# The last block of a feed-forward kernel: pieces of tiles, where small sums run, and who adds the residual

## The chip, the cores and the metric

The kernel runs on the 8 cores of one Trainium2 chip, each with its own half of one batch element; the cores don't exchange data. The metric is the device time of the slowest core in microseconds (us). A core has five engines with a queue of instructions each, worked off in order: TensorE (PE in the profile, PEld its weight loads), VectorE (DVE), ScalarE (ACT), GpSimd (POOL) and SyncE (SP). Sixteen DMA engines move data between HBM and SBUF; transfers are issued from the queues of SP, GpSimd or ScalarE. Matmuls write into PSUM, which has 8 banks of 128 x 512 float32. An instruction waits on semaphores that other engines count up.

## The reference, cut to what matters

```
x   = x + LN(attention(LN(x)))          # called x1 below
x   = x + LN(ffn(LN(x)))
ffn(x) = (silu(x gate_w' * gate_s) * (x up_w' * up_s)) down_w' * down_s
LN(x)  = (x - mean) / sqrt(var + 1e-5)
```

Rows have 2048 columns and the inner width is 5632. Each core holds 1024 rows. The change is in the last line alone: the product with down_w, the scale down_s, the layer norm of each row and the addition of x1.

## The kernel before, in words

The 1024 rows of a core are 8 tiles (`tt` 0 to 7) of 128 rows. After attention, x1 of each tile is written to the output tensor `y` in HBM (`x1`, L505, `spill`), and its layer norm is kept in SBUF. The feed-forward part then goes over 44 slices of 128 of the inner width (`gi`), in ten blocks: nine of 4 slices and a last one of 8 (`BLKS`). For a slice the gate and up products are made (L799), joined and gated into `hdn`. Then `down` multiplies `hdn` with the slices of down_w for each tile (`down_mm`, L830, the matmul at L837) into four banks of PSUM, and VectorE adds these 2048 columns to the float32 accumulator `acc` in SBUF (`acc_add`, L852).

In the last block (from L935) the down products of all 8 tiles follow one another: 8 slices x 4 banks = 32 matmuls a tile, bank after bank (`by_bank`), tiles 0, 2, 4, 6 into banks 0 to 3, the others into banks 4 to 7. Behind each tile come:

- `acc_add`: VectorE adds PSUM to `acc`;
- `scaled` (L970): VectorE multiplies by down_s (`dsB`) and sums the row (`accum_out`), one instruction with two SBUF operands and a short read of the accumulator;
- `squares` (L978): ScalarE squares the row and sums it; the written squares go to `junk`, so that one waits for the other;
- `means` (L986): VectorE makes minus the mean and minus the squared mean, 128 x 1 each; `variance` (L996): VectorE adds the mean square;
- `rstd` (L1002): ScalarE takes logarithm and exponential of the variance; `bias` (L1009): VectorE makes the bias, which holds the constant `cN` of the first layer norm;
- `normed` (L1015): ScalarE normalises the tile in place, 2048 wide;
- `add_up` (L1022): GpSimd issues an accumulating DMA that adds the tile to x1 in `y`.

The order on each queue is the order in which the program calls these helpers. For a tile `tt` below 6 (loop at L1050) `variance` and `rstd` of tile `tt - 1` stand ahead of `scaled(tt)`, and `bias`, `normed` and `add_up` of `tt - 1` behind `means(tt)`.

Tiles 6 and 7 are treated apart (from L1068). `part(tt, k)` adds, scales and squares one quarter, 512 columns, as soon as its bank is done. The four partial sums are added by `joined` and `joined_sq` (`reduce_sum` on VectorE). x1 of these two tiles has been read back from `y` into `x1r` (two DMAs on SP's queue, L962, when the last gate product is done); VectorE adds it and SP writes the sum (`store`, L1029). Tile 6 goes in two halves, tile 7 in four quarters. On VectorE's queue, the first half of tile 6's `store` stands ahead of `joined(7)`, and the second ahead of `bias(7)`. The last instruction of the program waits for all writes.

## Time and profile before

| | |
|---|---|
| median of 3 runs | 1055.78 us (1053.21 to 1227.72) |
| profiled execution | 1055.02 us, span of its slowest core (core 7) 1053.5 us |
| spans of the 8 cores | 1049.5 to 1053.5 us |
| busy: PE, DVE, ACT, POOL | 96%, 56%, 27%, 5% of the span |
| chain that ended last | PE 81%, DMA 5%, DVE 5%, ACT 5%, issue 3% |

The span goes from the first to the last instruction or transfer of a core; the 1.5 us that the execution is longer lie around it. Busy shares are means over stages with different limits. The chain of waits is followed back from what ended last, at each step to what released it. A wait is put down to the engine whose signal came last. In the timeline each row has start, duration, engine, line, operation, and, in brackets, how long the engine stood idle before it and for whom. ACT's and DVE's short READ_ACCUMULATOR instructions belong to the sums ahead of them.

### The profile page before, as it was taken

What the parts mean: (1) busy time and instruction counts of PE and PEld (TensorE: products, weight loads), DVE (VectorE), ACT (ScalarE), POOL (GpSimd) and SP (SyncE); (2) the same over time, 40 slices, a digit from 0 to 9 for tenths busy, and PEclk for the clock granted to TensorE, in tenths of its full rate; (3) what the DMA queues carried; (4) which work ended last, traced back from release to release, by engine and by line L of the source; (5) the groups of instructions that cost most, each with busy time, mean ns of one, the idle gap of its engine ahead of it and who ended that gap; (6) DMA issues with size and microseconds to landing.
All of it is one profiled execution on the core that took longest, in us unless ns stands there. A gap on an engine that the chain in (4) does not pass through costs nothing.

```text
span 1053.5 us, 12922 instructions; the slowest of 8 cores (1049.5 to 1053.5 us)
## 1 busy us (share of the span) xinstructions
PE 1006.6 (96%) x4868; PEld 461.8 (44%) x4868; DVE 591.6 (56%) x814; ACT 289.5 (27%) x427; POOL 52.1 (5%) x98
## 2 busy tenths in 40 slices
PE   2899999999999999999999999999999999999993
PEld 0345554444444444444444444444444444444441
DVE  3656667445646555654655555654555555555577
ACT  3555666622112012111112112111112121112266
...
GB/s 210 144 1 110 113 138 50 149 162 81 46 69 79 116 52 87 114 41 104 97 40 123 77 40 147 54 40 159 41 53 147 40 73 128 49 71 162 119 120 200
DMA packets 18636, 101.35 MB, mean 96 GB/s; under 512 B 2192, under 2 KB 2320, under 8 KB 9744
## 3 DMA queue, kind: packets, MB, share of 16 engines
...
q8 instruction: 40, 0.66, 0.3%
...
## 4 chain that ended last, share of the span: by engine, by line
PE 81%; DMA 5%; DVE 5%; ACT 5%; issue 3%; POOL 0%; DVEq 0%; ACTq 0%; SPq 0%; POOLq 0%
PE ps L799 45%; PE ps L837 28%; PE ps L443 4%; DMA dwb<-dw 3%; PE ps L412 2%; DMA wr<-gu 1%; DVE xr L508 1%; ACT lc L545 1%; DMA xr<-xtop 1%; ACT lc L468 1%; ACT pc L334 1%; PE ps L732 1%; ACT bop L340 1%; DVE acc L826 0%; DVE att L426 0%
## 5 line engine op out<-in xcount | busy, mean ns | idle before, releaser
L799 PE MATMUL ps<-bop,wr 128*128 128x512 bf16 x2352 | 520.0, 379 | 1.7 <-DMA wr<-gu 1.7
L799 PEld LDWEIGHTS ps<-bop,wr 128*128 128x128 bf16 x2352 | 229.9, 98 | 279.3 <-issue 2.5
L837 PE MATMUL ps<-dwb,hdn 128*128 128x512 bf16 x1344 | 307.2, 379 | 1.0 <-DMA dwb<-dw 0.9
L852 DVE TENSOR_TENSOR acc<-acc,ps 128x2048 f32<-128x2048 f32 x70 | 160.2, 2288 | 213.2 <-PE ps L837 213.2
L837 PEld LDWEIGHTS ps<-dwb,hdn 128*128 128x128 bf16 x1344 | 131.3, 98 | 160.5 <-issue 2.9
L772 ACT COPY tmp<-ps 128x512 f32<-128x512 f32 x126 | 73.3, 582 | 347.7 <-PE ps L799 347.7
L780 DVE TENSOR_TENSOR tmp<-tmp,ps 128x512 f32<-128x512 f32 x126 | 86.5, 686 | 92.1 <-ACT tmp L772 46.0
L759 DVE TENSOR_TENSOR wr<-wr 128x1024 bf16<-128x1024 bf16 x168 | 114.2, 686 | 8.2 <-DMA wr<-gu 3.7
L443 PE MATMUL ps<-att,xT 128*128 128x512 bf16 x512 | 117.4, 379 | 0.5 <-DVE xT L341 0.5
L710 ACT ACTIVATE sg<-tmp,cpks 128x512 bf16<-128x512 f32 x63 | 45.5, 722 | 239.7 <-DVE tmp L780 239.7
L443 PEld LDWEIGHTS ps<-att,xT 128*128 128x128 bf16 x512 | 49.5, 98 | 58.2 <-issue 1.0
L86 POOL DMA_DIRECT2D wr<-gu x44 | 23.5, 534 | 888.9 <-PE ps L799 625.6
L721 DVE SCALAR_TENSOR_TENSOR hdn<-tmp,cpks,sg 128x512 bf16<-128x512 f32 x63 | 47.3, 751 | 6.6
L412 PE MATMUL ps<-V,Xn 128*128 128x512 bf16 x128 | 36.2, 395 | 4.5 <-DVE att L426 1.9
L850 DVE COPY acc<-ps 128x2048 f32<-128x2048 f32 x8 | 18.3, 2292 | 25.4 <-PE ps L837 25.4
L721 DVE SCALAR_TENSOR_TENSOR hdn<-ps,cpks,sg 128x512 bf16<-128x512 f32 x25 | 18.6, 749 | 23.4 <-PE ps L799 11.1
L426 DVE TENSOR_SCALAR att<-ps 128x1024 bf16<-128x1024 f32 x16 | 19.6, 1225 | 19.8 <-PE ps L412 19.8
L710 ACT ACTIVATE sg<-ps,cpks 128x512 bf16<-128x512 f32 x25 | 17.1, 687 | 49.6 <-PE ps L799 46.5
L732 PE MATMUL ps<-bop,wr 128*128 128x512 bf16 x128 | 28.1, 379 | 0.0
L455 DVE SCALAR_TENSOR_TENSOR vp<-ps,sS,xr 128x512 f32<-128x512 f32 x32 | 23.3, 747 | 3.7 <-PE ps L443 3.7
L86 POOL DMA_DIRECT2D dwb<-dw x42 | 22.3, 550 | 17.1 <-ACT tmp L772 16.9
L981 ACT ACTIVATE junk<-acc 128x512 bf16<-128x512 f32 (+1 forms) x14 | 16.4, 1174 | 23.5 <-DVE acc L974 22.6
...
## 6 DMA issues: line engine op xcount, KB each, us to landing
wr<-gu POOLq DMA_DIRECT2D x44, 1024.0 KB, 9.7
...
xr<-x SPq DMA_DIRECT2D x8, 1024.0 KB, 6.1
y<-xr SPq DMA_DIRECT2D x8, 1024.0 KB, 3.9
y<-acc POOLq DMA_DIRECT2D x6, 1024.0 KB, 8.8
x1r<-y SPq DMA_DIRECT2D x2, 1024.0 KB, 6.0
...
xr<-xtop SPq DMA_DIRECT2D x4, 256.0 KB, 11.5
```

What stands on the lines that cost most here:

```text
L86: return self.put(eng, lambda e: e.dma_start(out, in_), after, sem, 16)
L412: t = pg.pe(lambda e, jt=jt: e.matmul(ps[:, bk, :], Xn[:, jt, nt * P:(nt + 1) * P], V[:, jt, q * MQ:(q + 1) * MQ], start=(jt == 0), stop=( ...
L443: t = pg.pe(lambda e: e.matmul(ps[:, bk, :], xT[:, i % 3, nt, :], att[:, nt, q * MQ:(q + 1) * MQ], start=(nt == 0), stop=(nt == NT - 1)), ...
L710: sl_t[q] = pg.ac(lambda e: e.activation(sg[:, q, :], src, AF.Silu, scale=cpk[:, C_GS + gi:C_GS + gi + 1]), [*after, *sg_free[q]])
L721: t = pg.dv(lambda e: e.scalar_tensor_tensor(hdn[:, gi % HS, h * MQ:(h + 1) * MQ], src, cpk[:, C_US + gi:C_US + gi + 1], sg[:, q, :], ALU. ...
L732: t = pg.pe(lambda e, ht=ht: e.matmul(ps[:, bk, :], wr[:, m, gi * 2 + ht // 8, (ht % 8) * P:(ht % 8 + 1) * P], bop[:, (B11, B21, B12, B22) ...
L759: cmb[(m, out)] = pg.dv(lambda e: e.tensor_tensor(u[:, out, :], u[:, in0, :], u[:, in1, :], op), [w_ld[m], *(cmb[(m, n)] for n in needs)])
L772: c = pg.ac(lambda e: e.copy(tmp[:, k, :], ps[:, bk, :]), [t, *tmp_free[k]])
L780: a = pg.dv(lambda e: e.tensor_tensor(tmp[:, k, :], tmp[:, k, :], ps[:, bk, :], ALU.add), [t, c])
L799: t = pg.pe(lambda e, c=c: e.matmul(ps[:, bk, :], wr[:, m % WS, ws, c * P:(c + 1) * P], bop[:, bs, c, :], start=(k in (1, 2, 5) and c == 0 ...
L837: t = pg.pe(lambda e, gi=gi, li=li, hc=hc: e.matmul(ps[:, banks[hc], :], hdn[:, gi % HS, tt * P:(tt + 1) * P], dw_at(gi)[:, hc * MQ:(hc + ...
L852: acc_t[tt] = pg.dv(lambda e: e.tensor_tensor(dst, dst, src, ALU.add), [t, acc_t[tt]])
```

## The change

Five things change in the last block.

- Tiles 0 to 2 are taken whole, 3 to 5 in two halves, 6 in a half and two quarters, 7 in four quarters (`PIECES`).
- The small sums (128 x 1) of tiles 0 to 6 run on GpSimd (`small`), those of tile 7 stay on VectorE. There are three for the means, as minus the mean is squared, negated and given epsilon in separate steps, and one or two more to join each sum of pieces (`total`).
- The mean square isn't added by itself: ScalarE's logarithm takes it as its input and the rest as its bias. The bias of the normalisation is made by ScalarE too, in `rstd`.
- x1 of tiles 0, 2, 7 and the second half of 6 is read back into `x1r` (four DMAs instead of two) and added by VectorE, with plain writes from SP's queue. Tiles 1, 3, 4, 5 and the first half of tile 6 are added by accumulating DMAs.
- The order of the calls is new: on ScalarE, `rstd` and `normed` of tile `tt - 1` stand between the squares of the first and second piece of tile `tt`; for tile 7 tile 6 is normalised in two halves, around the square of its second quarter.

```diff
--- before.py
+++ after.py
...
     rW = sb("rW", [P, DT])
     bW = sb("bW", [P, DT])
     nmW = sb("nmW", [P, DT])
-    wpart = sb("wpart", [P, 2, NQ])
-    qpart = sb("qpart", [P, 2, NQ])
+    wpart = sb("wpart", [P, DT, NQ])
+    qpart = sb("qpart", [P, DT, NQ])
+    mqW = sb("mqW", [P, DT])
     def views(size, *groups):
...
          ("bcb", [P, 2, 2, J], BF16), ("amixb", [P, 2, J], BF16),
          ("gT", [P, 2, J], BF16),
          ("Xn", [P, 2, D], BF16), ("V", [P, 2, D], BF16)],
-        [("x1r", [P, 2, D], F32), ("junk", [P, D], BF16)])
+        [("x1r", [P, 4, D], F32), ("junk", [P, D], BF16)])
     ((_, xT, xr), (wr, dwb), (dwx1, _, dsB, dwx0)) = views(
         67584,
         [("padB", [P, 22528 // 4], F32), ("xT", [P, 3, NT, P], BF16),
...
     part_t = {}
...
+    def acc_part(tt, ks, banks, name):
+        src = ps[:, banks[0]:banks[-1] + 1, :].rearrange("p a b -> p (a b)")
+        acc_t[(tt, name)] = pg.dv(lambda e: e.tensor_tensor(
+            acc[:, tt, ks], acc[:, tt, ks], src, ALU.add),
+            [part_t[banks[-1] % 4], acc_t[tt]])
+        for bk in banks:
+            tok_bank[bk] = (acc_t[(tt, name)],)
     def down_mm(b, tt, banks, order, sig):
...
     t = down_mm(b, 0, (0, 1, 2, 3),
                 [(li, hc) for li in (6, 7) for hc in range(4)], never)
     acc_add(b, 0, (0, 1, 2, 3), t)
-    x1_at = {6: 0, 7: 1}
+    x1_at = {0: 0, 2: 1, 6: 2, 7: 3}
     x1_ld = {}
-    for tt in (6, 7):
-        x1_ld[tt] = pg.dma("sync", f"xo{tt}", x1r[:, x1_at[tt], :],
...
+    for tt, s in x1_at.items():
+        lo = R if tt == 6 else 0
+        x1_ld[tt] = pg.dma("sync", f"xo{tt}", x1r[:, s, lo:],
+                           t_y.ap()[tt * P:(tt + 1) * P, lo:],
                            [spill[inv[tt]], w_free[NM - 1]])
     by_bank = [(li, hc) for hc in range(4) for li in range(BLKS[b])]
     w_t, sq_t, mq_t, vw_t, nm_t, rw_t, bw_t, nrm_t = ({} for _ in range(8))
     LAST = DT - 1
...
+    def scaled(tt, ks, s, name):
+        w_t[(tt, name)] = pg.dv(lambda e: e.scalar_tensor_tensor(
             acc[:, tt, ks], acc[:, tt, ks], 1.0, dsB[:, ks], ALU.mult,
...
+            ALU.mult, accum_out=s), [acc_t[(tt, name)], ds_ld])
+    def squares(tt, ks, s, name):
+        sq_t[(tt, name)] = pg.ac(lambda e: e.activation(
             junk[:, ks], acc[:, tt, ks], AF.Square, accum_out=s),
...
+            [w_t[(tt, name)], junk_t[0], w_free[NM - 1]])
+        junk_t[0] = sq_t[(tt, name)]
+    def small(tt, fn, after):
+        return pg.dv(fn, after) if tt == LAST else pg.put(
+            "gpsimd", fn, after, "GP")
     def means(tt):
         c = slice(tt, tt + 1)
...
+        nm_t[tt] = small(tt, lambda e: e.tensor_scalar_mul(
+            nmW[:, c], wsum[:, c], -1.0 / D), [w_t[(tt, None)]])
+        a = small(tt, lambda e: e.tensor_tensor(
+            mqW[:, c], nmW[:, c], nmW[:, c], ALU.mult), [nm_t[tt]])
+        mq_t[tt] = small(tt, lambda e: e.tensor_scalar(
+            vw[:, c], mqW[:, c], -1.0, EPS, ALU.mult, ALU.add), [a])
     def rstd(tt):
         c = slice(tt, tt + 1)
         a = pg.ac(lambda e: e.activation(
...
+            lnW[:, c], wsq[:, c], AF.Ln, scale=1.0 / D, bias=vw[:, c]),
+            [mq_t[tt], sq_t[(tt, None)]])
         rw_t[tt] = pg.ac(lambda e: e.activation(
             rW[:, c], lnW[:, c], AF.Exp, scale=-0.5), [a])
...
+        bw_t[tt] = pg.ac(lambda e: e.activation(
+            bW[:, c], nmW[:, c], AF.Identity, scale=rW[:, c],
+            bias=cN[:, c]), [nm_t[tt], rw_t[tt], cn_t[inv[tt]]])
+    def normed(tt, lo=0, hi=D):
+        c, ks = slice(tt, tt + 1), slice(lo, hi)
+        nrm_t[tt] = pg.ac(lambda e: e.activation(
             acc[:, tt, ks], acc[:, tt, ks], AF.Identity,
             scale=rW[:, c], bias=bW[:, c]), [bw_t[tt]])
...
+    def add_up(tt, hi=D):
         pg.put("gpsimd", lambda e: e.dma_start(
...
+            t_y.ap()[tt * P:(tt + 1) * P, :hi], acc[:, tt, :hi],
+            accum_op=ALU.add), [nrm_t[tt], spill[inv[tt]]], "ya", 16)
+    def store(tt, lo, hi):
         ks = slice(lo, hi)
         d = pg.dv(lambda e: e.tensor_tensor(
...
+            acc[:, tt, ks], acc[:, tt, ks], x1r[:, x1_at[tt], ks], ALU.add),
+            [nrm_t[tt], x1_ld[tt]])
+        pg.dma("sync", f"y{lo // MQ}", t_y.ap()[tt * P:(tt + 1) * P, ks],
                acc[:, tt, ks], [d])
+    def total(tt, out, parts, after):
+        n = len(PIECES[tt])
+        if tt == LAST:
+            return pg.dv(lambda e: e.reduce_sum(
+                out[:, tt:tt + 1], parts[:, tt, :], AX.X), after)
+        t = None
+        for k in range(1, n):
+            in0 = (parts[:, tt, 0:1] if k == 1 else out[:, tt:tt + 1])
+            t = small(tt, lambda e, k=k, in0=in0: e.tensor_tensor(
+                out[:, tt:tt + 1], in0, parts[:, tt, k:k + 1], ALU.add),
+                [*after, t])
+        return t
     def joined(tt):
...
+        w_t[(tt, None)] = total(tt, wsum, wpart,
+                                [w_t[(tt, len(PIECES[tt]) - 1)]])
         means(tt)
     def joined_sq(tt):
...
+        sq_t[(tt, None)] = total(tt, wsq, qpart,
+                                 [sq_t[(tt, len(PIECES[tt]) - 1)]])
+    def whole(tt):
+        acc_t[(tt, None)] = acc_t[tt]
+        scaled(tt, slice(0, D), wsum[:, tt:tt + 1], None)
+        squares(tt, slice(0, D), wsq[:, tt:tt + 1], None)
+        means(tt)
+    two, four = ((0, 1), (2, 3)), ((0, 0), (1, 1), (2, 2), (3, 3))
+    PIECES = {3: two, 4: two, 5: two, 6: ((0, 1), (2, 2), (3, 3)), 7: four}
+    def cols(tt, j):
+        lo, hi = PIECES[tt][j]
+        return slice(lo * MQ, (hi + 1) * MQ)
+    def taken(tt, j):
+        lo, hi = PIECES[tt][j]
+        acc_part(tt, cols(tt, j),
+                 [4 * (tt % 2) + k for k in range(lo, hi + 1)], j)
+    def summed(tt, j):
+        scaled(tt, cols(tt, j), wpart[:, tt, j:j + 1], j)
+        squares(tt, cols(tt, j), qpart[:, tt, j:j + 1], j)
     junk_t = [None]
...
+    for tt in range(DT):
+        banks = (0, 1, 2, 3) if tt % 2 == 0 else (4, 5, 6, 7)
         if tt > 0:
...
+            ends_at = [hi for lo, hi in PIECES.get(tt, ())]
+            t = down_mm(b, tt, banks, by_bank,
+                        lambda li, hc: hc in ends_at and li == BLKS[b] - 1)
+        if tt not in PIECES:
+            if tt > 0:
+                acc_add(b, tt, banks, t)
+                rstd(tt - 1)
+            whole(tt)
+            if tt > 0:
+                normed(tt - 1)
+            if tt == 2:
+                add_up(1)
+                store(0, 0, R)
+                store(0, R, D)
+            continue
+        taken(tt, 0)
+        summed(tt, 0)
+        if tt in (4, 5):
+            store(2, (tt - 4) * R, (tt - 3) * R)
+        taken(tt, 1)
+        rstd(tt - 1)
+        if tt < LAST:
             normed(tt - 1)
...
+            if tt > 3:
+                add_up(tt - 1)
+            summed(tt, 1)
+            for j in range(2, len(PIECES[tt])):
+                taken(tt, j)
+                summed(tt, j)
+            joined(tt)
+            joined_sq(tt)
     tt = LAST
...
+    normed(tt - 1, 0, R)
+    add_up(tt - 1, R)
+    summed(tt, 1)
+    normed(tt - 1, R, D)
+    for j in (2, 3):
+        taken(tt, j)
+        summed(tt, j)
     joined(tt)
     joined_sq(tt)
...
     rstd(tt)
...
+    store(tt - 1, R, R + MQ)
+    store(tt - 1, R + MQ, D)
     for k in range(4):
...
+        normed(tt, k * MQ, (k + 1) * MQ)
+        store(tt, k * MQ, (k + 1) * MQ)
     pg.put("sync", None,
            [(n, pg.count[n]) for n in ("ya", "y0", "y1", "y2", "y3")])
```

## Rows read from the trace of the kernel before

**Rows 1.** Cores view, the slowest: span, and mean granted TensorE clock.

```profile
core 7: 1053.5 us, clock 0.995
```

**Rows 2.** Chain of waits from 985 us: start, duration, what.

```profile
987.12 41.45 PE ps L837 x192
```

**Rows 3.** Timeline, the tail: start, duration, engine, line, operation, count, [idle before].

```profile
1036.59 0.59 PE L837 MATMUL ps<-dwx,hdn 128*128 128x512 bf16 x2
...
1041.12 0.68 DVE L826 TENSOR_TENSOR acc<-acc,ps 128x512 f32<-128x512 f32 x1
...
1043.18 0.63 ACT L981 ACTIVATE junk<-acc 128x512 bf16<-128x512 f32 x1
1043.71 0.19 ACT L981 ACTIVATION_READ_ACCUMULATOR junk<-acc 128x1 f32 x1
1043.78 0.15 DVE L1040 TENSOR_REDUCE wsum<-wpart 128x1 f32<-128x4 f32 x1
1043.94 6.15 SPq L86 DMA_DIRECT2D y<-acc  x6
1044.04 0.15 DVE L990 TENSOR_SCALAR nmW<-wsum 128x1 f32<-128x1 f32 x1
...
1044.52 1.22 DVE L1031 TENSOR_TENSOR acc<-acc,x1r 128x1024 f32<-128x1024 f32 x1
1044.70 0.29 ACT L1004 ACTIVATE lnW<-vw,eps_c 128x1 f32<-128x1 f32 x1 [0.80 <-DVE vw L998]
1045.08 0.20 ACT L1006 ACTIVATE rW<-lnW 128x1 f32<-128x1 f32 x1
1045.65 0.21 DVE L1011 SCALAR_TENSOR_TENSOR bW<-nmW,rW,cN 128x1 f32<-128x1 f32 x1
1045.96 2.93 ACT L1018 ACTIVATE acc<-acc,bW,rW 128x512 f32<-128x512 f32 x4 [0.68 <-DVE bW L1011]
1046.95 2.74 DVE L1031 TENSOR_TENSOR acc<-acc,x1r 128x512 f32<-128x512 f32 x4 [1.08 <-ACT acc L1018]
```

**Rows 4.** Waits, 988 to 1038 us: who waited for whom, total, times, longest.

```profile
DVE acc L852 <- PE ps L837: 8.9, 6, 1.8
...
DVE bW L1011 <- ACT rW L1006: 1.3, 1, 1.3
```

**Rows 5.** Groups of ScalarE's instructions by shape, 988 to 1054 us: busy, mean ns.

```profile
L1018 ACT ACTIVATE acc<-acc,bW,rW 128x2048 f32<-128x2048 f32 x7 | 14.5, 2078 | 0.0
L981 ACT ACTIVATE junk<-acc 128x2048 bf16<-128x2048 f32 x6 | 11.5, 1910 | 22.1 <-DVE acc L974 22.1
L981 ACT ACTIVATE junk<-acc 128x512 bf16<-128x512 f32 x8 | 5.0, 621 | 1.4 <-DVE wsq L1046 0.7 <-DVE acc L974 0.5
```

**Rows 6.** The same view, VectorE.

```profile
L974 DVE SCALAR_TENSOR_TENSOR acc<-acc,dsB 128x512 f32<-128x512 f32 x8 | 5.5, 692 | 0.8
...
L990 DVE TENSOR_SCALAR nmW<-wsum 128x1 f32<-128x1 f32 x8 | 1.2, 154 | 0.9
```

**Rows 7.** Timeline: ScalarE's normalisation of tile 0 and GpSimd's DMA behind it.

```profile
1002.55 2.08 ACT L1018 ACTIVATE acc<-acc,bW,rW 128x2048 f32<-128x2048 f32 x1
...
1005.29 0.88 POOL L1025 DMA_DIRECT2D y<-acc  x1 [30.91 <-ACT acc L1018]
```

**Rows 8.** Stretches: busy (count) of five engines, granted clock, DMA share, GB/s.

```profile
987.00:997.00 10.00, 10.00 (x48) 4.56 (x47) 7.39 (x8) 2.00 (x2) 0.00 (x0) 1.00 0.56 211
1018.00:1025.00 7.00, 7.00 (x34) 3.18 (x33) 5.13 (x8) 4.58 (x6) 0.85 (x1) 1.00 0.90 152
1040.00:1047.00 7.00, 0.00 (x0) 0.00 (x0) 5.47 (x15) 5.34 (x11) 0.00 (x0) 0.68 0.99 202
1047.00:1054.00 7.00, 0.00 (x0) 0.00 (x0) 2.66 (x4) 1.89 (x3) 0.00 (x0) 0.50 0.75 258
```

**Rows 9.** DMA issues, 1037 to 1038 us: count, KB, us to landing.

```profile
y<-acc POOLq DMA_DIRECT2D x1, 1024.0 KB, 11.2
```

**Rows 10.** DMA issues, 1025 to 1027 us.

```profile
y<-acc POOLq DMA_DIRECT2D x1, 1024.0 KB, 8.4
```

More of the change, by code:

```diff
@@ L1015, in normed @@
-    def normed(tt, k=None):
-        c = slice(tt, tt + 1)
-        ks = slice(0, D) if k is None else slice(k * MQ, (k + 1) * MQ)
-        nrm_t[(tt, k)] = pg.ac(lambda e: e.activation(
+        bw_t[tt] = pg.ac(lambda e: e.activation(
[4 more added lines that the diff above has]
+        nrm_t[tt] = pg.ac(lambda e: e.activation(
@@ L1019, in normed @@
             acc[:, tt, ks], acc[:, tt, ks], AF.Identity,
             scale=rW[:, c], bias=bW[:, c]), [bw_t[tt]])
-    def add_up(tt):
+    def add_up(tt, hi=D):
         pg.put("gpsimd", lambda e: e.dma_start(
-            t_y.ap()[tt * P:(tt + 1) * P, :], acc[:, tt, :],
-            accum_op=ALU.add), [nrm_t[(tt, None)], spill[inv[tt]]], "ya", 16)
-    def store(tt, lo, hi, after, sem):
+            t_y.ap()[tt * P:(tt + 1) * P, :hi], acc[:, tt, :hi],
+            accum_op=ALU.add), [nrm_t[tt], spill[inv[tt]]], "ya", 16)
@@ L1049, in build_nc @@
+    def summed(tt, j):
+        scaled(tt, cols(tt, j), wpart[:, tt, j:j + 1], j)
+        squares(tt, cols(tt, j), qpart[:, tt, j:j + 1], j)
     junk_t = [None]
-    for tt in range(DT - 2):
+    for tt in range(DT):
+        banks = (0, 1, 2, 3) if tt % 2 == 0 else (4, 5, 6, 7)
         if tt > 0:
-            banks = (0, 1, 2, 3) if tt % 2 == 0 else (4, 5, 6, 7)
-            t = down_mm(b, tt, banks, by_bank, never)
-            acc_add(b, tt, banks, t)
-        acc_t[(tt, None)] = acc_t[tt]
-        if tt >= 1:
-            variance(tt - 1)
-            rstd(tt - 1)
-        scaled(tt)
-        squares(tt)
-        means(tt)
-        if tt >= 1:
-            bias(tt - 1)
-            normed(tt - 1)
-            add_up(tt - 1)
@@ L1068, in part @@
-    def part(tt, k):
-        acc_part(tt, k, 4 * (tt % 2) + k)
-        scaled(tt, k)
-        squares(tt, k)
-    tt = LAST - 1
-    down_mm(b, tt, (0, 1, 2, 3), by_bank,
-            lambda li, hc: li == BLKS[b] - 1)
-    part(tt, 0)
-    part(tt, 1)
-    variance(tt - 1)
-    rstd(tt - 1)
-    part(tt, 2)
-    bias(tt - 1)
-    normed(tt - 1)
-    add_up(tt - 1)
-    part(tt, 3)
-    joined(tt)
-    tt = LAST
-    down_mm(b, tt, (4, 5, 6, 7), by_bank,
-            lambda li, hc: li == BLKS[b] - 1)
@@ L1089, in build_nc @@
-    part(tt, 0)
-    joined_sq(tt - 1)
-    variance(tt - 1)
-    rstd(tt - 1)
-    part(tt, 1)
-    bias(tt - 1)
-    normed(tt - 1)
-    part(tt, 2)
-    part(tt, 3)
-    store(tt - 1, 0, R, nrm_t[(tt - 1, None)], "y0")
+            ends_at = [hi for lo, hi in PIECES.get(tt, ())]
[13 more added lines that the diff above has]
+            continue
@@ L1099, in build_nc @@
+    add_up(tt - 1, R)
[4 more added lines that the diff above has]
+        summed(tt, j)
     joined(tt)
     joined_sq(tt)
-    variance(tt)
     rstd(tt)
-    store(tt - 1, R, D, nrm_t[(tt - 1, None)], "y1")
-    bias(tt)
+    store(tt - 1, R, R + MQ)
+    store(tt - 1, R + MQ, D)
     for k in range(4):
-        normed(tt, k)
-        store(tt, k * MQ, (k + 1) * MQ, nrm_t[(tt, k)], f"y{k}")
+        normed(tt, k * MQ, (k + 1) * MQ)
+        store(tt, k * MQ, (k + 1) * MQ)
```

43 lines of the change are left out of this document (removed).

## The prediction

> **What bounds the kernel now.** Core 7 is the slowest [rows 1], so its trace is read. The chain of waits comes first: from 987.1 us one piece, 41.5 us of down projection, 192 matmuls at 0.216 us [rows 2]. All of the last block up to there is TensorE, at full clock and untouched by the change. One bank takes 8 matmuls, 1.73 us, a tile 6.91 us. The last matmul ends at 1037.2 [rows 3] and the span at 1053.5, so what this change can move is a tail of 16.3 us.
>
> The timeline of the tail comes next [rows 3]. The last add out of PSUM starts at 1041.12, 3.9 us after its matmul: VectorE is behind, because its in-order list waits 1.3 us for ScalarE's exponential of tile 5 [rows 4], holds small sums between the quarters, and adds a 1.22 us x1 half before it takes the last sums. ScalarE's last square starts at 1043.18, the logarithm at 1044.70. The bias is ready to be computed at about 1045.4 but starts at 1045.65, behind the second x1 half. Then four quarters follow, and the last store is issued at about 1049.8 (the row of the six issues ends at 1050.1, one takes 0.3). It lands at the end of the span, some 3.4 us later.
>
> The DMA engines are the second bound: 0.99 busy from 1040 to 1047 and 0.75 to the end [rows 8]; the last accumulating write takes 11.2 us [rows 9].
>
> **The change, part by part.**
>
> Tiles 0 to 5. VectorE waits 8.9 us in six adds for TensorE [rows 4], about 1.7 us in each of the later ones. It loses four small sums a tile (three of 0.15 like L990 [rows 6], and L1011 with 0.21 [rows 3]), and in the stages of tiles 4 and 5 gains one x1 half of 1.22 us [rows 3]. Two half tiles cost 2 x (1.3 + 1.2) = 5.0 (a half add and a half scaling, like the x1 half's 1.22 and the start of the next), with the x1 half 6.2 us of 6.91: covered. The stage of tile 2 gets two halves, 2.44 us, against the 1.7 of slack and the small sums' 0.4; followed through in order, VectorE is 1.7 us late at the first half of tile 4, 0.9 at tile 5's and level at tile 6's. TensorE takes a tile's banks again 6.9 us after it left them, and the add needs 2.3 of these, so it notices nothing under 4 us. Cost: nothing.
>
> x1 loads: four instead of two, 3.5 MiB instead of 2, on SP's queue, which has nothing else to do until the first store. Two took 0.56 of 10 us of the DMA engines [rows 8], 2.8 us per MiB, so four take 9.8 and end at about 998. Tile 0's is first and is needed at 1007. The four stores of tiles 0 and 2 (two MiB, 5.6 us of DMA) go out between 1008 and 1026 on SP's queue and replace two accumulating writes, each 0.90 of 7 us, 6.3 us [rows 8]. All of that is hidden. The last block's accumulating writes fall from 6 to 4.5 MiB.
>
> VectorE at the end. In halves and quarters, with bias and variance gone from it, VectorE reaches the last bank when TensorE does: start at 1037.3 instead of 1041.12, 3.8 us sooner. Alone this would be the gain. It isn't, for ScalarE and GpSimd come behind it.
>
> The small sums. On tile 6, two adds join the three piece sums, three make the means, two join the squares: seven dependent steps on GpSimd, each waiting on its own semaphore, and behind them in line ScalarE's logarithm of tile 6, behind which three squares of tile 7 are queued. On tiles 4 and 5 it is five steps, and ahead of all of them stands the accumulating write, 0.9 us of GpSimd's time (0.86 by L1025 [rows 7]), which itself waits for ScalarE's normalisation. No row shows a small GpSimd sum. VectorE's dependent step is 0.26 us (L1040 to L990 [rows 3]), ScalarE's 0.38 (logarithm to exponential [rows 3]). The upper row is far off: GpSimd starts its DMA 0.66 us after the ScalarE instruction before it ended (1004.63 to 1005.29 [rows 7]), which with 0.15 for the sum would be 0.8 a step. Since the steps follow each other without a new engine, I take 0.35, between the two near rows, and keep 0.1 (VectorE's L990 and L992 side by side) and 0.8 as ends. The Trainium skill (GPSIMD Engine Reference, section Performance versus the Vector engine) has a long two-input add at 1.96 times VectorE's time; no run here shows it, and on a step of 0.26 it would make 0.51 us, an estimate that gives 1056.8 instead of my sum.
>
> The sum, with s for a step. ScalarE start to start: normalise 2048 wide 2.0 us, 512 wide 0.71 (2.93 less 0.80, over 3), squares 0.61, and 0.80 before another square, which waits for the read of the accumulator too, 0.19; 1024 wide by interpolation 1.14 and 1.04 [rows 3, 5]. Logarithm, exponential and bias on ScalarE, each with 0.1 for its signal: 0.39 + 0.30 + 0.38 (the bias taken as long as the logarithm) = 1.07.
> - VectorE has scaled tile 4's first half at 1017.4, ScalarE squares it and, after 1.07, has tile 3 normalised at 1021.9: write at 1022.6. Then 0.9, five steps to 1025.2, 1.07, 2.1 for tile 4, and 0.6 to GpSimd: write at 1029.0.
> - The same again, 0.9, five steps, 1.07, 2.1 and 0.6: tile 5's write at 1035.4 (before: 1037.3).
> - 0.9, then seven steps: 1038.75. The three squares that ScalarE has until then end at 1037.1, so it stands for 1.6 us.
> - Plus 1.07: 1039.8. Half of tile 6 1.14, a square 0.61, the other half 1.14, two squares 0.80 each: 1044.3. The last square starts at 1043.5; before, 1043.18. The 3.8 us of VectorE are lost again in this queue.
> - Tail: reduction 0.25, logarithm to bias 1.07, normalised quarter to VectorE 0.95 to 0.99 [rows 3], three quarters 0.71, the add 0.78: issue at 1049.5. Here the change wins what it promises: square to first normalised quarter takes 2.1 us instead of 2.8, as the bias no longer waits behind the x1 half.
> The same bookkeeping on the kernel before gives 1050.2 against 1049.8, so I take off 0.4: 1049.1, 0.7 us sooner. The landing, 3.4 us, shrinks a little with less queued ahead, by 0.3. Span 1052.5, 1.0 us less. Of the 1055.02 us of the profiled execution (span 1053.5), that leaves **1054.0**; the median of the runs shown is 1055.78, 0.8 above that execution.
>
> Each 0.1 in s is worth 1.7 us above 0.3 (5 + 5 + 7 steps in line), less below, where ScalarE has its own work.
>
> The DMA floor. After the change the last stretch holds 1 MiB and half a MiB accumulating (6.3 + 3.15) and 1.5 MiB plain (4.2): 13.65 us. With the write of tile 5 issued at 1034.5 and 1 us to its first data, that is 1049.2, and 0.9 to the end: 1050.1. The same count before, two accumulating MiB from 1034.4, where tile 3's write lands (1026.0 and 8.4 [rows 10]), and two plain, gives 1052.6 + 0.9 = 1053.5, the span. So no case gains over 3.4 us.
>
> **Rivals.**
> Small sums are cheap (chance 0.28). With s at 0.2 or less ScalarE has its own work until 1036.8, the last issue comes by 1047.2, and the DMA floor holds the end at 1050.1: **1051.6**. For it: VectorE's small sums need 0.15. Against: GpSimd's slow reaction [rows 7].
>
> GpSimd steps decide (0.2). From s above 0.4 the sums of tile 6 cost more than the tail wins; at 0.5 the issue is at 1051.7 and the time **1056.8**, at 0.6 it is 1058.4. The place is ScalarE idle ahead of tile 6's logarithm, 4 us at 0.5 instead of 1.6. For it: the 0.66 us [rows 7]; against: nothing but the near rows.
>
> VectorE and GpSimd shut each other out (0.17). If a small sum can't start while VectorE runs an instruction with two SBUF operands (the scaling, 0.69 us in every 1.73 at the end, the x1 adds of 1.22), each chain waits for one to three such instructions. Counted through in order at 0.35 a step, tile 4's sums lose 2.5 us to two scalings of halves (1.2 each), tile 5's another 1.7, and tile 6's about none; tile 5's write slips to 1039, tile 6's logarithm to 1042.5, the last issue to 1053.3: **1058.5**. It decides from s about 0.2 up. The trace has no GpSimd read of SBUF beside them, so it says nothing. The Trainium skill (SBUF — State Buffer, section Who interferes with whom) states exactly this: such a VectorE instruction "contends with a GpSimd instruction that reads SBUF", and the later one waits for the whole of the other.
>
> My forecast, small change either way, has 0.35. The change does what it says; there is no case for that.
>
> **The numbers.** 1054.0 us. Low: the floor case 1051.6 less 1.8, the profiled execution above the lowest run shown (1053.21): 1050. High: steps of 0.5 and shutting out together put the issue at 1056.3, 1061. About 2% is what a measurement can tell; 21 us is more than the tail of 16.3 can give back, and slower by that needs steps over 1.2 us or both rivals near 0.9. Chances: faster by over 2% 0.01, within 0.96, slower 0.03.
>
> **What would show it.** The first PSUM add of the last bank near 1037.3 (VectorE's step). Spacing of the small sums on GpSimd (0.35), and whether they start at ends of scaling instructions (shutting out). ScalarE's idle before tile 6's logarithm (1.6 us), and its last square (1043.1). Tile 5's write at 1035. Logarithm to first quarter 1.1 us. DMA share from 1036 to the end. I'm wrong if TensorE stalls in the last block, or if the last store lands much later than 3.4 us after its issue.

## The result, and the profile after

The changed kernel takes 1056.33 us (median of 13 runs) against 1053.94 for the kernel before (13 runs). Two of the 13 runs of each kernel are slow ones (in those of after the cores of one die show a lower clock, 0.84 to 0.97), and without them the medians are 1056.23 and 1053.91; every time and ratio below is taken without such runs. The ratio is 1.0021, 95% interval 1.0014 to 1.0029: 2.3 us slower. Forecast were 1054.0 us and, from the profiled execution, a gain of 1.0.

A caution on the size: the profiled execution of before [rows 1] took 1055.02 us, 1.1 above its kernel's median, and that of after 1055.71 us, 0.5 below its own. Their spans differ by 0.7 us only. The last matmul of the slowest core ends at 1037.2 in the one and 1034.7 in the other, and it moves like this from core to core and execution to execution (1031 to 1039 in the traces of this study). What hardly moves is the work behind it: counted from the core's own last matmul, the logarithm of tile 6, for one, starts within 0.02 us of the same time on all 8 cores of these two kernels (0.07 at most in the others). So times below with a sign count from the core's last matmul. The *last issue* is the start of the DMA issue of the last store; where the text says how long this store takes to land, the time runs from there to the end of the core, 0.3 us behind the landing itself.

The cores view of after, its slowest core (compare [rows 1]):

```profile
core 4: 1054.2 us, clock 0.992
```

The timeline of its tail (start, duration, engine, line, operation, idle before), the counterpart of [rows 3]:

```profile
1034.06 0.59 PE L840 MATMUL ps<-dwx,hdn 128*128 128x512 bf16 x2
...
1034.76 0.69 DVE L827 TENSOR_TENSOR acc<-acc,ps 128x512 f32<-128x512 f32 x1 [0.23 <-PE ps L840]
...
1035.39 0.90 POOL L1023 DMA_DIRECT2D y<-acc  x1 [3.90 <-ACT acc L1016]
...
1036.04 0.47 POOL L1044 TENSOR_TENSOR wsum<-wpart 128x1 f32<-128x1 f32 x1
...
1036.66 0.19 POOL L1044 TENSOR_TENSOR wsum<-wsum,wpart 128x1 f32<-128x1 f32 x1
...
1037.01 0.22 POOL L995 TENSOR_SCALAR nmW<-wsum 128x1 f32<-128x1 f32 x1 [0.16 <-POOL wsum L1044]
...
1037.38 0.19 POOL L997 TENSOR_TENSOR mqW<-nmW 128x1 f32<-128x1 f32 x1
1037.73 0.19 POOL L999 TENSOR_SCALAR vw<-mqW 128x1 f32<-128x1 f32 x1 [0.16 <-POOL mqW L997]
1038.00 0.19 POOL L1044 TENSOR_TENSOR wsq<-qpart 128x1 f32<-128x1 f32 x1
1038.34 0.19 POOL L1044 TENSOR_TENSOR wsq<-wsq,qpart 128x1 f32<-128x1 f32 x1
1038.62 0.29 ACT L1005 ACTIVATE lnW<-wsq,vw 128x1 f32<-128x1 f32 x1 [1.53 <-POOL wsq L1044]
...
1039.30 0.39 ACT L1010 ACTIVATE bW<-nmW,cN,rW 128x1 f32<-128x1 f32 x1
...
1043.46 0.63 ACT L982 ACTIVATE junk<-acc 128x512 bf16<-128x512 f32 x1
...
1044.54 0.29 ACT L1005 ACTIVATE lnW<-wsq,vw 128x1 f32<-128x1 f32 x1 [0.35 <-DVE wsq L1039]
...
1045.16 4.94 SPq L86 DMA_DIRECT2D y<-acc  x6
1045.22 0.39 ACT L1010 ACTIVATE bW<-nmW,cN,rW 128x1 f32<-128x1 f32 x1
1045.70 2.93 ACT L1016 ACTIVATE acc<-acc,bW,rW 128x512 f32<-128x512 f32 x4
1046.69 2.74 DVE L1030 TENSOR_TENSOR acc<-acc,x1r 128x512 f32<-128x512 f32 x4 [1.00 <-ACT acc L1016]
```

VectorE does what the change wants: its last add out of PSUM starts 0.11 us after the last matmul (1034.76) instead of 3.94. But on GpSimd the seven small sums of tile 6 stand behind tile 5's write (1035.39) and run from 1036.04 to 1038.34. Only then can ScalarE take tile 6's logarithm, at +3.97 us (before: +1.49), and tile 7's squares queue behind that: the last one starts at +8.81 (before +5.99), the last store is issued at +15.0 on most cores (before +12.57).

| from the last matmul, us | before | after |
|---|---|---|
| last add out of PSUM | +3.94 | +0.11 |
| tile 6's logarithm | +1.49 | +3.97 |
| last square | +5.99 | +8.81 |
| tile 7's logarithm | +7.5 | +9.9 |
| last store issued | +12.57 | +15.0 to 15.4 |
| end of the core | +15.8 to 18.9 | +18.5 to 20.1 |
| from last issue to the end | 3.2 to 6.3 | 3.5 to 5.1 |

The waits of after from 988 to 1050 us (who waited for whom, total, times, longest), beside [rows 4]:

```profile
DVE wsq L1039 <- ACT junk L982: 6.8, 1, 6.8
ACT lnW L1005 <- POOL wsq L1044: 5.6, 3, 2.5
```

ScalarE now stands 5.6 us for GpSimd's last small step, once each in tiles 4, 5 and 6. VectorE stands 6.8 us for ScalarE's last square. It has little else to do, but the two adds of tile 6's second half, whose normalisation ends at 1042.76, are behind that wait on its queue until 1044.39, and so are their writes; what this costs was not tested.

The stretches (busy and count of PE, PEld, DVE, ACT, POOL, granted clock, DMA share, GB/s), beside [rows 8]:

```profile
1029.00:1036.00 7.00, 5.60 (x26) 2.35 (x24) 5.90 (x13) 5.06 (x9) 2.55 (x7) 1.00 1.08 171
1036.00:1043.00 7.00, 0.00 (x0) 0.00 (x0) 0.88 (x6) 5.10 (x12) 2.59 (x9) 0.57 0.99 159
1043.00:1050.00 7.00, 0.00 (x0) 0.00 (x0) 4.11 (x7) 4.91 (x11) 0.00 (x0) 0.50 1.00 161
```

From 1029 us on the DMA engines are full to the last stores. The share is the summed time of the packets over that of 16 engines, so it can pass 1. The accumulating writes of tile 5 and of half of tile 6 (count, KB, us to landing), beside [rows 9]:

```profile
y<-acc POOLq DMA_DIRECT2D x1, 1024.0 KB, 9.7
```

```profile
y<-acc POOLq DMA_DIRECT2D x1, 512.0 KB, 7.8
```

Half a MiB took 7.8 us. It was issued at +7.1 and landed at +14.9; only then do the last plain writes have the engines for themselves.

### The profile page after: what moved, and what is told of

Read it like the earlier page. It is cut to its first block, busy times and chain, and to the rows that moved or that the text cites. A ratio compares the mean times of both kernels' runs of the same rounds, so it can differ in the third digit from the quotient of the medians.

```text
span 1054.2 us, 12886 instructions; the slowest of 8 cores (1051.0 to 1054.2 us)
## 1 busy us (share of the span) xinstructions
PE 1002.4 (95%) x4772; PEld 462.0 (44%) x4868; DVE 591.9 (56%) x793; ACT 293.5 (28%) x440; POOL 61.9 (6%) x128
## 4 chain that ended last, share of the span: by engine, by line
PE 80%; ACT 6%; issue 4%; DVE 4%; DMA 4%; POOL 1%; DVEq 0%; ACTq 0%; POOLq 0%; SPq 0%
PE ps L800 46%; PE ps L840 26%; PE ps L444 4%; PE ps L413 3%; DMA dwb<-dw 2%; DVE xr L509 1%; DMA wr<-gu 1%; ACT lc L546 1%; DMA xr<-xtop 1%; ACT lc L469 1%; ACT pc L335 1%; ACT acc L1016 1%; PE ps L733 1%; ACT bop L341 1%; DVE acc L1030 0%
## 5 line engine op out<-in xcount | busy, mean ns | idle before, releaser
L855 DVE TENSOR_TENSOR acc<-acc,ps 128x2048 f32<-128x2048 f32 x67 | 153.2, 2287 | 207.9 <-PE ps L840 207.9
L427 DVE TENSOR_SCALAR att<-ps 128x1024 bf16<-128x1024 f32 x16 | 19.6, 1224 | 20.1 <-PE ps L413 20.1
L86 POOL DMA_DIRECT2D dwb<-dw x42 | 22.3, 550 | 16.8 <-ACT bop L341 16.6
L413 PEld LDWEIGHTS ps<-V,Xn 128*128 128x128 bf16 x128 | 12.2, 102 | 23.7 <-issue 13.5
```

What stands on the lines that cost most here:

```text
L86: return self.put(eng, lambda e: e.dma_start(out, in_), after, sem, 16)
L413: t = pg.pe(lambda e, jt=jt: e.matmul(ps[:, bk, :], Xn[:, jt, nt * P:(nt + 1) * P], V[:, jt, q * MQ:(q + 1) * MQ], start=(jt == 0), stop=( ...
L855: acc_t[tt] = pg.dv(lambda e: e.tensor_tensor(dst, dst, src, ALU.add), [t, acc_t[tt]])
```

## Why the sums were late: the rows

The timeline of after around tile 4's small sums:

```profile
1020.62 1.22 DVE L1030 TENSOR_TENSOR acc<-acc,x1r 128x1024 f32<-128x1024 f32 x1
...
1020.83 1.06 POOL L1044 TENSOR_TENSOR wsum<-wpart 128x1 f32<-128x1 f32 x1
...
1023.08 1.25 DVE L977 SCALAR_TENSOR_TENSOR acc<-acc,dsB 128x1024 f32<-128x1024 f32 x1
1023.34 1.04 POOL L1044 TENSOR_TENSOR wsq<-qpart 128x1 f32<-128x1 f32 x1
...
1024.47 0.29 ACT L1005 ACTIVATE lnW<-wsq,vw 128x1 f32<-128x1 f32 x1 [2.47 <-POOL wsq L1044]
```

A small GpSimd sum lasts 0.19 to 0.22 us, and a dependent one starts 0.35 us after the one ahead (1037.38, 1037.73). Here one lasts 1.06 and one 1.04 us. Each starts while VectorE runs an instruction that reads two SBUF operands, and ends about 0.05 us after it (the VectorE instructions end at 1021.84 and 1024.33, the sums at 1021.89 and 1024.38). This is the mechanism of the rival that had a chance of 0.17; call it *shutting out*. By the Trainium skill (SBUF — State Buffer, section Who interferes with whom) the later of the two waits for the whole of the other; the trace agrees.

Two explanations can now be told apart. **Theory A:** there are two bounds, nearly equal. The chain (VectorE, GpSimd, ScalarE) fixes the last issue, and it is lengthened by shutting out. The DMA backlog of accumulating writes sets a floor under the end that a sooner issue doesn't pass. **Theory B:** one bound only, the chain, with a fixed time from the last issue to the end. Most experiments move one of the two, some move both. (An expectation uses letters of its own where it says so.)

## Experiments: the chain

**1. Scaling with one SBUF operand.** VectorE multiplies by a constant; `down_s` is left out of the result. (Indices and brackets of the code are shortened here.)

```
-        w_t[...] = scalar_tensor_tensor(acc, acc, 1.0, dsB[:, ks], mult, mult, accum_out=s)
+        w_t[...] = tensor_scalar(acc, acc, 0.05, 0.0, mult, add, accum_out=s)
```

> The changed kernel, but VectorE's scaling multiplies by a constant instead of the tile of down_s, so that it has one SBUF operand instead of two (the scale down_s is left out of the output). If GpSimd's small sums are held up by VectorE's two-operand instructions: no small sum lasts over 0.6 us any more except beside the x1 adds, tile 6's logarithm starts 1.6 to 2.2 us after the last matmul (changed kernel: 3.97), the last store is issued 12.8 to 13.3 us after it (changed: 15.0), and the time falls by about 2 us, to the level of the kernel before. If the length of the chain of steps alone counts (seven at 0.35): nothing of this moves by more than 0.3 us. If the fp32 scaling gets faster with one operand, VectorE's pieces shorten, but TensorE sets their pace.

Measured: 1055.83 us, ratio to before 1.0019 (1.0008 to 1.0029). The timeline of core 4, the same place in tile 4:

```profile
1019.80 1.22 DVE L977 TENSOR_SCALAR_CACHE_REDUCE acc<-acc 128x1024 f32<-128x1024 f32 x1
1020.04 0.19 POOL L1044 TENSOR_TENSOR wsq<-qpart 128x1 f32<-128x1 f32 x1
...
1020.33 0.29 ACT L1005 ACTIVATE lnW<-wsq,vw 128x1 f32<-128x1 f32 x1 [1.62 <-POOL wsq L1044]
```

The scaling is as long (1.22 us), and the sum under it now takes 0.19 us instead of 1.04. Tile 6's logarithm comes at +2.42 instead of +3.97. Shutting out by the scaling is therefore real and costs 1.55 us of the chain. The last issue, at +15.0 to +15.4, now comes at +13.6 to +14.2. (The sum beside tile 2's x1 half, which still has two operands, lasts 1.07 us here too.) Yet the time doesn't fall by a measurable amount, against the 2 us of the expectation: the last store now takes 4.7 to 6.1 us to land, before this edit 3.5 to 5.1, and the cores end at +18.4 to +20.3 as they did. That speaks against theory B.

**2. GpSimd only writes.** Constants are stored in place of the small sums, so mean and variance are left out and GpSimd reads nothing; each constant still waits for the one ahead. ScalarE's logarithm takes the last piece's squares and epsilon instead (that part of the edit isn't shown).

```
-            "gpsimd", fn, after, "GP")
+            "gpsimd", lambda e: e.memset(nmW[:, tt:tt + 1], 0.0),
+            [*after, ("GP", pg.count.get("GP", 0))], "GP")
```

> The changed kernel with each small sum of tiles 0 to 6 on GpSimd replaced by a memset of the same 128 x 1 size with the same waits, which reads no SBUF (mean and squared mean are left out, and of pieces only the last one's squares are used). Shutting out of reads: no step lasts over 0.4 us, the last store is issued 12.8 to 13.3 us after the last matmul. If any use of GpSimd beside VectorE costs, writes as well: it stays near 15.0.

Measured, one run: 1057.78 us, on a core whose last matmul ended as late as 1039.0, so the time says little and the trace must be read. Core 3, tile 4's five steps beside an x1 half, which has two SBUF operands:

```profile
1020.75 1.22 DVE L1033 TENSOR_TENSOR acc<-acc,x1r 128x1024 f32<-128x1024 f32 x1
1020.91 1.29 POOL L990 MEMSET nmW<- 128x1 f32 x5
```

Five constants take 1.29 us there, 0.26 each: writes aren't held, so it is GpSimd's reads that are shut out. Tile 6's logarithm is at −0.36, the last issue at +10.7 to +11.7, more than 3 us sooner on every core and sooner than expected. The last store then needs 6.6 to 9.1 us to land, and the cores end at +17.2 to +19.8. Some 4 us less of chain give 0.7 us less at the end (mean of the 8 cores, 18.65 against 19.37).

**3. One more small step** on each tile's GpSimd chain: a second `mqW = nmW * nmW` behind the first.

> The changed kernel with one more dependent small product on GpSimd in the means of tiles 0 to 6. If the steps of tiles 4, 5 and 6 stand in line on the path, the last store is issued three times 0.35 = 1.05 us later, 16.05 us after the last matmul, up to 17 where a step meets a two-operand instruction; tile 4's accumulating write 0.35 later, tile 5's 0.7. If they are hidden by ScalarE's own work: no change.

Measured, one run: 1057.26 us; logarithm +4.65, last issue +15.7, both 0.7 later. That is two steps of 0.35 and not three. Counted from tile to tile, tile 3's write doesn't move, tile 4's goes out 0.24 us later, tile 5's 0.35 and tile 6's logarithm 0.68. So tile 6 pays its step in full, and tiles 4 and 5 pay one between them. The step was rightly sized at 0.35, and it counts where it isn't hidden; in tile 4 it falls among sums that are held anyway.

**4. The small sums on VectorE**, as five to seven separate instructions.

```
-        return pg.dv(fn, after) if tt == LAST else pg.put("gpsimd", fn, after, "GP")
+        return pg.dv(fn, after)
```

> The changed kernel with the small sums of all tiles on VectorE, at the same places in the program. If GpSimd as such is the cost: steps of 0.26 us instead of 0.35 and more, the last store 12 to 13.5 us after the last matmul. If what matters is what a queue waits for: VectorE now waits for ScalarE's squares at the end of each tile (joined squares, behind a 2048-wide normalisation), the last PSUM add starts 8 to 11 us after the last matmul instead of 0.1, and the last store is issued at 18 to 20: slower than the changed kernel by 3 to 5 us.

Measured: 1061.43 us, ratio 1.0071 (1.0051 to 1.0091). VectorE's last add out of PSUM slips from +0.11 to +11.3, for it now waits 5.8 us in four places for ScalarE's squares, with adds and scalings queued behind; tile 6's logarithm comes at +9.34, the last issue at +20.34. That is the second reading of the expectation, somewhat dearer than it said. With this list of sums and this order, moving them off VectorE was right. Experiment 9 changes list and order.

**5. Tiles 0 and 2 accumulating again** (x1 added by VectorE to half of tile 6 and tile 7 only).

```
-    x1_at = {0: 0, 2: 1, 6: 2, 7: 3}
+    x1_at = {6: 2, 7: 3}
...
+            if tt == 1:
+                add_up(0)
...
-        if tt in (4, 5):
-            store(2, (tt - 4) * R, (tt - 3) * R)
...
-            if tt > 3:
-                add_up(tt - 1)
+            add_up(tt - 1)
```

> The changed kernel with tiles 0 and 2 written by accumulating writes again (x1 added by VectorE only to half of tile 6 and tile 7). Theory A (the DMA backlog): accumulating traffic grows by 2 MiB, but earlier in the stage, where the DMA engines stand idle for some 6 us between -18 and -12 us before the last matmul; the 1.9 MiB of plain writes and reads goes from the busy stretch; the end comes 0 to 1 us sooner or later than in the changed kernel. Theory C (VectorE's two-operand additions of x1 at tiles 2, 4 and 5 stretch the GpSimd steps and so delay every later tile): tile 6's logarithm comes at +2.5 to +3.2 us after the last matmul instead of +3.97, the last issue at +13.8 to +14.5 instead of +15.0. Theory B (only the seven last small steps count): logarithm and last issue unchanged within 0.3 us. Time 1055.0 to 1056.5 us.

Measured: 1056.61 us, ratio 1.0028 (1.0017 to 1.0038); logarithm +4.33, issue +15.2 to +15.4. The theory that the x1 additions delay the chain in total (C in the expectation) fails: without them tile 6's logarithm is 0.36 us later. The timeline of core 4, tile 3's sums:

```profile
1012.24 1.23 DVE L977 SCALAR_TENSOR_TENSOR acc<-acc,dsB 128x1024 f32<-128x1024 f32 x1
1012.29 1.23 POOL L997 TENSOR_TENSOR mqW<-nmW 128x1 f32<-128x1 f32 x1
```

The accumulating write of tile 2 now stands ahead of these sums on GpSimd, and a sum that then falls under a scaling is held for 1.23 us. Tile 3's write goes out at −12.9 instead of −14.5. What one side of the exchange wins, the other loses: which sum is held depends on where it falls. So this run doesn't tell the x1 halves' own price.

## Experiments: the DMA backlog

**6. Tile 6 written whole by plain writes**, as before the change. Accumulating traffic is 4 MiB instead of 4.5 and ends with tile 5's write.

```
-        lo = R if tt == 6 else 0
+        lo = 0
...
-    add_up(tt - 1, R)
...
     joined(tt)
+    store(tt - 1, 0, R)
     joined_sq(tt)
```

> The changed kernel, but tile 6 is written whole by plain writes after VectorE has added x1 to it (as in the kernel before); its accumulating write of 0.5 MiB at 7.1 us after the last matmul is gone, 1 MiB accumulating traffic less is not: tiles 1, 3, 4, 5 accumulate, 4 MiB less 0. Theory A (the DMA engines' backlog sets the end): the last accumulating write is now tile 5's, issued at +0.7 us and landed at about +10.5, and the last store lands 3.0 to 3.5 us after its issue instead of 3.5 to 5.1; the end of a core comes 17.8 to 18.8 us after its last matmul instead of 18.5 to 20.1; time about 1055.3 us. Theory B (the chain of ScalarE and small sums alone sets the end): last issue unchanged at +15.0, end unchanged at 18.5 to 20.1, time 1056.2 us.

Measured: 1055.20 us, ratio 1.0012 (1.0002 to 1.0023). The last issue is nearly unchanged (+14.9), the landing falls to 3.2 to 4.0 us, the cores end at +18.0 to +18.8. By the medians this is 1.0 us less, as theory A has it (the intervals of the two ratios overlap a little). The ends say the same: 0.9 us less in the mean, of which the issue has 0.2.

**7. Plain writes for all accumulating ones** (x1 is left out of those tiles), with the changed kernel and with experiments 1 and 2.

```
-            t_y.ap()[tt * P:(tt + 1) * P, :hi], acc[:, tt, :hi],
-            accum_op=ALU.add), [nrm_t[tt], spill[inv[tt]]], "ya", 16)
+            t_y.ap()[tt * P:(tt + 1) * P, :hi],
+            acc[:, tt, :hi]), [nrm_t[tt], spill[inv[tt]]], "ya", 16)
```

> The changed kernel with its accumulating writes made plain ones from the same queue: x1 is left out of the output of tiles 1, 3, 4, 5 and half of 6, and a MiB costs the DMA engines some 2.8 us instead of 6.3. Theory A (DMA backlog behind the chain): last issue unchanged at +15.0 us after the last matmul, the last store lands 2.3 to 3.2 us after it, end at 17.3 to 18.2 us instead of 18.5 to 20.1, time about 1054.5 us. Theory B (chain alone): end unchanged, 1056.2 us.

> Scaling on VectorE by a constant (one SBUF operand instead of two; the vector down_s is left out), and accumulating writes made plain (x1 left out of those tiles). With accumulating writes the same scaling brought the last issue 1.4 us sooner and the time did not fall. Theory A (it was the DMA backlog that ate it): now issue at +13.3 to +13.6 us after the last matmul, the last store lands 3.2 us later, end at 16.6 to 16.9, time 1.2 to 1.5 us under the kernel with plain writes alone (1054.88): 1053.5 us. Theory B (the gain in the chain is spent elsewhere): 1054.9 us.

> As the run in which GpSimd only stored constants in place of the small sums (the mean and the variance are left out of the result) and ScalarE's last issue came at +10.7 us, but with accumulating writes made plain (x1 left out as well). Theory A (the DMA backlog kept that run's end at 17.2 to 18.7 us after the last matmul although the last issue came 4.3 us sooner): without it the last store lands 2.5 to 3.5 us after its issue, the end comes at 13.2 to 14.5 us, time about 1050.5 us. Theory B (the last store has a fixed price of its own and there is no backlog): the landing stays at 6.4 to 7.8 us after issue, end at 17 us, time 1054 to 1057 us.

| kernel | last issue | end | time, us | ratio to before |
|---|---|---|---|---|
| changed | +15.0 to 15.4 | +18.5 to 20.1 | 1056.23 | 1.0021 (1.0014 to 1.0029) |
| one operand | +13.6 to 14.2 | +18.4 to 20.3 | 1055.83 | 1.0019 (1.0008 to 1.0029) |
| plain writes | +14.8 | +17.9 to 18.9 | 1054.88 | 1.0010 (1.0001 to 1.0020) |
| both | +12.9 | +15.8 to 17.2 | 1053.28 | 0.9993 (0.9983 to 1.0002) |
| plain, GpSimd only writes | +10.4 | +13.3 to 14.6 | 1050.50 | 0.9967 (0.9955 to 0.9978) |

With accumulating writes the one-operand scaling changed the time by 0.4 us, with plain ones by 1.6. (Plain writes also help the chain a little: GpSimd's issue of one lasts 0.62 us and not 0.90, and tile 6's logarithm comes 0.2 us sooner.) For GpSimd without reads the stretches show it best; first with accumulating writes (core 3, last matmul at 1034.80), then with plain ones (core 2, 1034.86):

```profile
1028.80:1034.80 6.00, 6.00 (x28) 2.55 (x26) 5.09 (x12) 4.95 (x10) 1.54 (x8) 1.00 1.10 135
1034.80:1040.80 6.00, 0.01 (x1) 0.00 (x0) 2.66 (x9) 5.23 (x12) 0.85 (x1) 0.67 1.10 184
1040.80:1046.80 6.00, 0.00 (x0) 0.00 (x0) 3.46 (x6) 3.52 (x6) 0.00 (x0) 0.50 1.06 158
```

```profile
1028.80:1034.80 6.00, 6.00 (x29) 2.55 (x26) 5.15 (x12) 5.19 (x11) 1.23 (x8) 1.00 0.37 154
1034.80:1040.80 6.00, 0.07 (x1) 0.00 (x0) 2.93 (x10) 5.20 (x11) 0.53 (x1) 0.85 0.38 154
1040.80:1046.80 6.00, 0.00 (x0) 0.00 (x0) 3.19 (x5) 3.31 (x5) 0.00 (x0) 0.50 0.90 248
```

The same chain, the same bytes of output: the DMA share is 1.1 in the one and 0.37 in the other until the last stores, and the end comes at 1053.1 and at 1048.5. The changed kernel with plain writes alone, core 3:

```profile
1028.80:1034.80 6.00, 6.00 (x30) 2.65 (x27) 5.21 (x13) 4.33 (x8) 2.29 (x6) 1.00 0.42 175
1034.80:1040.80 6.00, 0.31 (x2) 0.00 (x0) 2.19 (x9) 3.95 (x11) 2.31 (x8) 0.72 0.43 176
```

The share is 0.42 where the changed kernel had 1.08. The time from the last issue to the end isn't fixed: it runs from 2.9 us to 9.1 over these runs, long where accumulating writes are queued. Theory B is refuted.

**8. The kernel before with plain writes.**

> The kernel before with its six accumulating writes made plain (x1 left out of tiles 0 to 5). Theory A: its last issue stays at +12.6 us after the last matmul, the landing falls from 3.2 to 6.3 us to 3.0 to 4.2 (3.2 on the cores whose last matmul ends late), the end is at 15.8 us on those cores as before, so the slowest core gains 0 to 0.5 us: 1053.3 to 1053.9 us. So before, the chain alone set the slowest core's end, and the change's 2.4 us of later issue explain the whole loss. Theory B (before was held by the DMA backlog): 1 us or more sooner, 1052.9 us or less.

Measured: 1052.51 us, ratio 0.9989 (0.9978 to 0.9999), so some 1.2 us sooner (0.1 to 2.3). The issue stays at +12.57. The cores end at +15.3 to +16.3; those with a late last matmul, one of each pair, at +15.3 to +15.7, where before they ended at +15.8 to +16.8. The 0 to 0.5 us of the expectation's theory A were too few: the backlog costs the kernel before about as much as it costs the changed one (1.4 us each by the medians). Between the two kernels with plain writes the medians differ by 2.4 us and the last issues by 2.2; with accumulating writes it is 2.3 and 2.4. (The plain ones were timed at different times, each beside runs of before; by their ratios they differ by 2.2 us, each ratio being good to about 1 us.) So the loss is that of the later issue, with or without backlog.

**9. A version made from this.** No small sum on GpSimd, and few on VectorE: the mean and its negative straight from two piece sums, the constant part of the variance from the first piece's squares, a fused product, and ScalarE's logarithm takes the last piece's squares itself. Each tile is normalised and written directly behind its own logarithm. Tiles 0 to 5 accumulate, tiles 6 and 7 are written plain; tile 6 comes in two halves. The edit is long; its operations in short, without the code around them:

```
+        nm = tensor_scalar(nmW, w0, w1, -1.0 / D, add, mult)      # VectorE
+        pm = tensor_scalar(mqW, w0, w1, 1.0 / D, add, mult)
+        q  = tensor_scalar(lnW, q0, 1.0 / D, EPS, mult, add)
+        vw = scalar_tensor_tensor(vw, nmW, mqW, lnW, mult, add)
+        rW = activation(q1, Ln, scale=1.0 / D, bias=vw)           # ScalarE
...
+            rstd(tt, ...); normed(tt); add_up(tt)    # of tile tt, not of tile tt - 1
```

> A version made from what the runs showed: no small sum on GpSimd. VectorE makes them in three or four instructions a tile (mean and its negative straight from the two piece sums, the constant part of the variance from the first piece's squares, one fused product), and ScalarE's logarithm takes the last piece's squares itself. Each tile is normalised and written right after its own logarithm, not one tile later; tiles 3 to 6 in halves, tile 7 in quarters; x1 is added by VectorE to tiles 6 and 7 only. Worked out in order from the durations of the two traces: accumulating writes at -37.5, -30.6, -23.7, -18.1, -12.4 and -6.0 us from the last matmul, last add out of PSUM at +2.2, tile 6's logarithm at -2.9, tile 7's at +5.0, last issue at +10.0. Theory A (chain, then the DMA backlog): the last accumulating write is 6 us sooner than before and lands by +4 to +6, 2 MiB of plain writes follow, so the last store lands 3.2 us after its issue: end at 13.2 us after the last matmul against 15.8 to 18.9 before, time about 1051 us, ratio 0.997. Theory B (GpSimd or DMA work sets the end whatever ScalarE does): end as before at 15.8 or later, 1053.5 us or more.

Measured: **1050.03 us**, ratio 0.9962 (0.9949 to 0.9975), some 3.9 us under before (whose median beside it was 1053.88) and 6.2 under the changed kernel. Its slowest core and its timeline (last matmul ends at 1036.08):

```profile
core 5: 1048.5 us, clock 0.995
```

```profile
1031.95 0.21 DVE L994 TENSOR_SCALAR nmW<-wpart 128x1 f32<-128x1 f32 x1
...
1032.08 0.20 DVE L996 TENSOR_SCALAR mqW<-wpart 128x1 f32<-128x1 f32 x1
1032.20 0.14 DVE L1002 TENSOR_SCALAR lnW<-qpart 128x1 f32<-128x1 f32 x1
...
1032.47 0.22 DVE L1004 SCALAR_TENSOR_TENSOR vw<-nmW,mqW,lnW 128x1 f32<-128x1 f32 x1
...
1033.23 0.29 ACT L1010 ACTIVATE rW<-qpart,vw 128x1 f32<-128x1 f32 x1
...
1035.49 0.59 PE L840 MATMUL ps<-dwx,hdn 128*128 128x512 bf16 x2
...
1038.35 0.68 DVE L827 TENSOR_TENSOR acc<-acc,ps 128x512 f32<-128x512 f32 x1
...
1040.99 0.29 ACT L1010 ACTIVATE rW<-qpart,vw 128x1 f32<-128x1 f32 x1 [0.28 <-DVE vw L1004]
...
1043.13 2.74 DVE L1032 TENSOR_TENSOR acc<-acc,x1r 128x512 f32<-128x512 f32 x4 [1.16 <-ACT acc L1021]
```

The four small instructions start within 0.52 us, since three of them don't depend on each other. Logarithm at −2.85 (worked out: −2.9), last add out of PSUM +2.27 (+2.2), tile 7's logarithm +4.9 (+5.0), last issue +9.87 (+10.0). The last accumulating write goes out at −6.0 and lands at +4.4 to +6.2, and the last store needs 2.5 to 3.7 us to land. The end lies at +12.4 to +13.5. This kernel moves both bounds: against before the last issue comes 2.7 us sooner and the last accumulating write 6 us. Its parts were not undone one by one, so how the 3.9 us divide among them is not shown.

## Why the prediction was wrong

The step that failed is the term of the small sums: five, five and seven steps of 0.35 us were taken to run undisturbed beside VectorE, and the rival that said otherwise was held for less likely. Its steps in order, with times against the last matmul:

- **VectorE's last add at +0.1** was right (+0.11), and so was TensorE's undisturbed work (the stretch of after with PE busy 5.60 of 7 us is the one in which the last matmul ends).
- **A step of 0.35 us** was right to the second digit where nothing holds it. The ratio 1.96 of the Trainium skill (GPSIMD Engine Reference, section Performance versus the Vector engine) is for long instructions; between these small ones it is 0.35 to 0.26 start to start, some 1.3.
- **The writes and tile 6's logarithm.** Tile 3's write was forecast at −14.6 and went out at −14.49. Tile 4's was forecast at −8.2 and came at −6.4, tile 5's at −1.8 and came at +0.7, tile 6's logarithm at +1.6 and came at +3.97. This is the failing step. Of the 2.4 us, 1.55 are the scaling's (experiment 1). About 0.6 more is the first sum of tile 4 under an x1 half, 1.06 us where the first sum behind a DMA issue elsewhere takes 0.47 (read from rows, not undone alone: experiment 5, which took the x1 half away, changed GpSimd's queue as well). The last 0.3 stand ahead of tile 4's `mqW`, which starts 0.66 us after `nmW` (1022.05, 1022.71) in place of 0.37, in experiment 1 too; what holds it is open. In experiment 1's kernel the time from tile 4's write to tile 5's is as forecast: 6.38 us, forecast 6.4. The rival's own count (logarithm at +5.3, 1058.5 us) was too dear, by 1.3 us in the logarithm.
- **ScalarE's stand of 1.6 us before that logarithm** was 1.53. That is luck, as its earlier work was late as well.
- **From the logarithm to the last issue** the forecast has 10.75 us less 0.4; it was 11.0. The bias on ScalarE takes 0.39 + 0.09 us and not 0.38, and it comes twice. The 0.4 was taken off because the same count on before came out 0.4 too long; it doesn't carry over and here only adds to the miss. Logarithm to first quarter, 1.1 us, was 1.16.
- **The last issue at +11.9** came at +15.0, 3.1 us later, which is 2.4 + 0.3 + 0.4.
- **The landing** was to shrink by 0.3 us, which from issue to end of core is 3.7 less 0.3. It was 3.5 to 5.1.
- **The DMA floor at +12.9** (1050.1) was too low by more than 4 us: experiment 2 has the ends at +17.2 to +19.8. The floor was counted from tile 5's write, as though tile 4's had landed, and with that write at 1034.5, where the forecast's own chain has 1035.4. But tile 3's goes out at −14.5 onto engines that had stood partly idle (share 0.70 from −18 to −12), and from there 3.5 MiB accumulate and 2 to 2.5 MiB are plain (tile 2's first half, issued at −18.8, lands at −13.2). By the forecast's own rates that is 22 us and 6 to 7, with 1 us to the first data and 0.9 at the end some +15 to +16.5 at the soonest. The traces are still later, by 1 to 5 us, and this rest is open. The landings show the queue: in experiment 2 the MiB of tiles 3 to 5 take 9.5 to 16.2 us each. The forecast took the sum of traffic to matter ("from 6 to 4.5 MiB"); the two tiles turned plain were early ones, whose traffic had room.

So the direction failed on the chain: the loss of 2.3 us goes with a last issue 2.4 us later, and it stays when no write accumulates. "No case gains over 3.4 us" rested on a floor that was too low. Even with small sums that nothing holds, a gain is unlikely: experiment 2 (one run) issues its last store 1.9 us sooner than the kernel before, and its cores with a late last matmul still end at +17.2 to +19.0, those of before at +15.8 to +16.8.
